# Loading order in the first expert stage: the fourth expert's weights behind the third's, the fifth's ahead of four raw attention pieces

## What is computed

```python
x = x + 0.5 * _L0_ffn_ref(_layernorm(x), gate_w, gate_b, w1, b1, w2, b2)
x = x + _L0_attn_ref(_layernorm(x), Wq, Wk, Wv, Wa, Wg, Wo, ln1..., W1, b1, W2, b2, ln2...)
x = x + 0.5 * _L0_ffn_ref(_layernorm(x), gate_w, gate_b, w1, b1, w2, b2)
```

## Time and profile before

| What | us |
|---|---|
| median of 3 runs | 725.04 (722.64 to 755.42) |
| profiled execution, its own time | 718.21 |
| profiled execution, span from first to last instruction | 716.5 |
| PE busy in the span | 644.8 (90%) |

### The profile page before, as it was taken

How to read it: one execution, slowest core, us unless ns; L and a number is a source line. 1 busy time by engine, 2 the same in 40 slices (tenths; PEclk the granted TensorE clock), 3 DMA queues, 4 the chain that set the end, 5 groups by cost and what they waited for, 6 DMA issues and landing times. The chain is left out here.

```text
span 716.5 us, 11537 instructions
## 1 busy us (share of the span) xinstructions
PE 644.8 (90%) x4307; PEld 572.1 (80%) x4311; DVE 478.7 (67%) x1059; ACT 451.1 (63%) x811; POOL 195.1 (27%) x290
## 2 busy tenths in 40 slices
PE   8999899987779899899999899999996789799993
PEld 5468799565669899799799798898886789489993
DVE  6663500256788989989989989988989776520001
ACT  3425244049689798898899898897797143244440
POOL 6150101320023134235236126215224121420112
PEclk9999999999879999999999999999998798799998
DMA  7959990242001210220121021011011095117700
GB/s 227 339 167 364 306 326 23 72 161 74 29 1 60 75 41 5 73 74 6 70 75 45 31 75 51 24 45 46 0 45 45 1 339 190 52 38 242 250 24 25
DMA packets 48864, 74.07 MB, mean 103 GB/s; under 512 B 4662, under 2 KB 40587, under 8 KB 48744
## 3 DMA queue, kind: packets, MB, share of 16 engines
q1 hardware_dynamic: 44456, 59.84, 25.5%
q0 software_dynamic: 4352, 13.49, 5.3%
HBM read 62.45 MB, written 15.20 MB: 108 GB/s over the span
## 5 line engine op out<-in xcount | busy, mean ns | idle before, releaser
L1639 PE MATMUL bank<-zt_h,w_in_h 128*128 128x512 f32 x192 | 81.4, 424 | 9.6 <-DVE zt_l L1298 5.0
L1639 PE MATMUL bank<-yt_h,w_h 128*128 128x256 f32 x256 | 75.6, 295 | 7.2 <-DVE yt_l L1423 6.4
L982 PE MATMUL bank<-xdt,ring 128*128 128x160 f32 x512 | 75.8, 308 | 4.7 <-DMA ring<-in_L_ffn_w 3.6
L784 DVE SCALAR_TENSOR_TENSOR xo<-bank,gate,xg 128x256 f32<-128x256 f32 x20 | 9.2, 482 | 104.8 <-PE bank L1009 104.8
L982 PEld LDWEIGHTS bank<-xdt,ring 128*128 128x128 f32 x512 | 73.4, 197 | 5.3 <-DMA ring<-in_L_ffn_w 3.8
L1640 PE MATMUL bank<-zt_l,w_in_h 128*128 128x512 f32 x192 | 77.1, 402 | 0.0
L1641 PE MATMUL bank<-zt_h,w_in_l 128*128 128x512 f32 x192 | 76.9, 401 | 0.0
L1639 PE MATMUL bank<-w_h,ht_h 128*128 128x256 f32 x256 | 74.3, 290 | 0.0
L995 PE MATMUL bank<-hid,ring 128*128 128x160 f32 x512 | 72.8, 300 | 1.5 <-DVE idx_s L768 0.7
L1641 PE MATMUL bank<-yt_h,w_l 128*128 128x256 f32 x256 | 73.6, 288 | 0.0
L1640 PE MATMUL bank<-yt_l,w_h 128*128 128x256 f32 x256 | 73.4, 287 | 0.0
(11 more groups left out here) (249 smaller groups left out, 1628.1 us busy)
## 6 DMA issues: line engine op xcount, KB each, us to landing
ring<-in_L_ffn_w SPq DMA_DIRECT2D x32, 1024.0 KB, 9.4
xc<-in_L_attn_x SPq DMA_DIRECT2D x8, 512.0 KB, 4.3
z_mid<-zb POOLq DMA_DIRECT2D x8, 512.0 KB, 3.4
zr<-z_mid SPq DMA_DIRECT2D x16, 256.0 KB, 2.9
xr<-x_mid SPq DMA_DIRECT2D x16, 256.0 KB, 3.6
out<-xq POOLq DMA_DIRECT2D x16, 256.0 KB, 4.2
zb<-x_mid SPq DMA_DIRECT2D x7, 512.0 KB, 5.4
xc<-in_L_attn_W SPq DMA_DIRECT2D x4, 512.0 KB, 8.5
```

The lines of the kernel that those rows point to most:

```text
L784: V.scalar_tensor_tensor(xo[:, a % GT, :], bank[6 + a % 2][:, 0:D], gate[:, a:a + 1], xg[:, a, :], ALU.mult, ALU.add).then_inc(xo_ready, 1)
L982: ins = T.matmul(bank[b][:, 0:CAP], w1_of(s)[:, k, m * P:(m + 1) * P], xdt[:, k, e * CAP:(e + 1) * CAP], start=k == 0, stop=k == KD - 1)
L1639: T.matmul(out, left[0], right[0], start=start, stop=False)
```

## The change

Three things move in `sync_program` of the first expert half, and only there. Nothing that PE, DVE, ACT or POOL execute changes.

1. Expert 3's two DMAs stand right behind expert 2's. The wait for gathers 0 and 1 stood ahead of them and now stands behind them, ahead of `wo_f` and pieces 0 to 3.
2. The copy stands where it stood: behind pieces 0 to 3 and a wait for gathers 0 to 4.
3. Pieces 4 and 5 follow the copy as before. Then come the wait for down 0 and expert 4, and behind these pieces 6 to 9. Expert 5 follows.

```diff
+        def raw_loads(sp, start, stop):
+
+            for n in range(start, stop):
+                if n >= RB:
+                    sp.wait_ge(raw_done, n + 1 - RB)
+                sp.dma_start(raw_view(n), pieces[n][0]).then_inc(raw_in[n % RB], 16)
+
...
-                if first and e == GE - 1:
-                    sp.wait_ge(xg_in[0], 16)
-                    sp.wait_ge(xg_in[1], 16)
                 sp.dma_start(w1_of(s), ew1[e].rearrange("(k p) f -> p k f", p=P)).then_inc(w_in[s], 16)
                 sp.dma_start(w2_of(s), ew2[e].rearrange("(m p) d -> p m d", p=P)).then_inc(w_in[s], 16)
                 if first and e == GE - 1:
 
                     sp.wait_ge(tp_ready, NB * KD)
                     sp.wait_ge(var_ready, NB)
+                    for a in TURN_IN[0]:
+                        sp.wait_ge(xg_in[a], 16)
                     wo = dense_src[5]
                     sp.dma_start(dense["wo_f"][:], wo.rearrange("(k p) n -> p k n", p=P)).then_inc(wo_in, 16)
-                    for n, (piece, _, _) in enumerate(pieces):
-                        if n >= RB:
-                            sp.wait_ge(raw_done, n + 1 - RB)
-                        sp.dma_start(raw_view(n), piece).then_inc(raw_in[n % RB], 16)
-                        if n == RB - 1:
-                            for a in range(GT):
-                                sp.wait_ge(xg_in[a], 16)
-                            sp.dma_start(dst, copy_from).then_inc(copied, 16)
+                    raw_loads(sp, 0, RB)
+                    for a in range(GT):
+                        sp.wait_ge(xg_in[a], 16)
+                    sp.dma_start(dst, copy_from).then_inc(copied, 16)
+                    raw_loads(sp, RB, RB + 2)
+                if first and e == GE:
+                    raw_loads(sp, RB + 2, len(pieces))
```

## The result

The changed kernel is slower: 726.57 us median of 20 runs (724.62 to 730.32), against 723.06 us for the kernel before (median of 20 runs, the three shown at first among them). The ratio is 1.0056, with a 95% interval of 1.0037 to 1.0074. (Ratios and intervals here are estimated from all the runs, so they differ a little from the quotient of two medians, here 1.0048.) Its profiled execution took 724.62 us.

What follows compares the result with a forecast made beforehand. PE, busy for 90% of the span, was taken as the bound, with late expert 4 weights costing a wait and slow clock at up 4. That 5.49 us, all else nothing, took 725.04 to 719.5 us; range 711 to 729.

Steps and rivals of the forecast that it cites:

- What bounds the kernel, and expert 4: At up 4, PE waits for expert 4's late weights, then runs at a slow clock; loading them earlier wins 5.49 us.
- the 3.71 us of waiting: Part of the expert 4 term: up 4 would start at 85.02 us and not at 88.73.
- The 1.78 us of slow clock: Part of the expert 4 term: without the pause before up 4, PE keeps its clock and wins another 1.78 us.
- Issue and landing of expert 4: On SP's queue, expert 4 goes out at about 67.4 us; its second half lands between 78.6 and 83.4, before 85.0.
- Pieces 6 to 9 at nothing: DVE's split before `xo` of tile 0 comes 5.6 us later, covered by downs and ups: cost nothing, otherwise 5.6 us.
- Expert 5's load as the narrowest place: Ahead of up 5: expert 5 lands at the latest at 92.9 us and is wanted at 93.9, so it holds.
- Expert 3 at nothing: Expert 3 lands at 43.4 us, hardly meeting the first gathers: cost taken as nothing, bounds nothing to 4.2 us.
- The copy's place: Before down 0, the copy's packets now overlap gathers 7 to 9: taken as nothing, upper end 5.5 us.
- the upper bound of the same paragraph: Last gathers held back until the copy is done, near 67 us, putting down 0 off by 5.5 us.
- case C: Last gathers held until the copy's packets are through, down 0 late: 7.3 us lost against 5.5 won, 726.8 us, chance 0.16.
- When the copy's packets begin: On SP's queue, the copy's packets begin at about 54 us, 5.6 us sooner than before.

Runs made afterwards that it cites:

- first pair of traces: Profiles of the kernel before and of the changed kernel as first measured: medians 723.06 and 726.57 us.
- experiment 3: Kernel before with only expert 4 moved ahead of pieces 6 to 9, expert 3 at its old place: 718.14 us, ratio 0.9911.
- experiment 12: Kernel before with expert 4 early, expert 3 at its old place, copy behind all ten gathers, repeated on a third chip: 715.47 us, ratio 0.9915.
- second pair: The kernel before and the changed kernel, both unchanged, run again on a third chip: 722.51 and 725.96 us.
- experiment 1: Changed kernel, but the copy waits for all ten gathers and not for five: 715.79 us, ratio 0.9886 against the kernel before.
- 11: Changed kernel with the copy behind all ten gathers, repeated on a third chip: 716.98 us, ratio 0.9927 against the kernel before.
- experiment 10: Changed kernel, unchanged, repeated on a third chip: 725.96 us, ratio 1.0045 against the kernel before.
- 2: Changed kernel with only expert 3 early, expert 4 behind all ten raw pieces again: 725.17 us, ratio 1.0038 against the kernel before.
- 4: Changed kernel with the copy cut into rows of 4 KB and not 64 KB (two DMAs): 720.59 us, ratio 0.9961 against the kernel before.
- 5: Kernel before with one edit, the copy waits for all ten gathers: 725.82 us, ratio 1.0011.
- 7: Changed kernel, but the copy waits for gathers 0 to 6, two more: 721.86 us, ratio 0.9986 against the kernel before.
- 8: Kernel before with expert 4 early, expert 3 at its old place, copy behind all ten gathers, on the second chip: 724.48 us, ratio 0.9987.

## Why the prediction was wrong

**What bounds the kernel, and expert 4.** Right. With expert 4 ahead of pieces 6 to 9, PE's wait for `ring` was gone in every profile. The term was 5.49 us, and 5.50 was measured in the first pair of traces. Experiments 3 and 12, where the gathers cost at most 0.4 us, measured 0.9911 and 0.9915 over the whole run, 6.1 to 6.4 us. Of its two parts, the 3.71 us of waiting is firm. The 1.78 us of slow clock is not: in the second pair it is not there (up 4 took 4.61 us in the kernel before), and the term is (94.11 - 77.13) - 13.26 = 3.72 us.

**Issue and landing of expert 4.** In the changed kernel it was issued at 77.75, not 67.4, since down 0 was late. In experiment 1 it was issued at 69.20, with down 0 1.82 us later than in the first trace. That is the 67.4 expected, moved by the same amount. Its second half, issued at 69.61, landed 12.3 us later, at 81.9, inside the bounds.

**Pieces 6 to 9 at nothing.** Right: PE has no wait for `xo` in any of the profiles. **Expert 5's load as the narrowest place** was right too. It was worked out to hold by 1 us. It held in the changed kernel, and in experiment 12, with the copy issued at 60.32, it failed by 1.01 us.

**Expert 3 at nothing.** Right for gathers 0 and 1 (3.6 and 2.7 us, as before), and its second half landed at 31.63 + 12.0 = 43.6, where 43.4 was worked out. Experiment 12 against 11 shows no value of its own either.

**The copy's place.** Here the prediction failed, in the sentence "I take nothing: the tenth gather alone would land at 53.99 + 2.7 = 56.7, 4.8 us before it is wanted, which is more than one 64 KB packet takes". It priced one turn for each gather. A gather needs three, and so the term put at nothing measured 6.85 us in the first pair of traces (14.02 - 7.17) and 7.86 in the second (15.02 - 7.16), with 2.02 and 1.38 us of slow clock in down 0 behind it. The last gather came in with the end of the copy. That was the upper bound of the same paragraph (5.5 us; its own sum, 54 + 13.8, is 67.8 and not 67, which makes it 6.3), and the case C built on it: 7.3 us lost against 5.5 won, 726.8 us, chance 0.16. The mechanism of C, its place and its sign are what happened. Its size was too small: in the second pair down 0 starts 71.75 - 63.80 = 7.95 us later and then takes 1.38 us more, so 9.33 lost against 3.72 won, 5.6 us at the end of that stretch. Over the whole run the medians differ by 3.5 us in both pairs (726.57 - 723.06 and 725.96 - 722.51). In the second pair's traces 1.86 of the 5.6 us come back at the start of attention, since there the kernel before has a wait that the changed one has not:

```profile
145.96 0.41 DVE L1289 TENSOR_TENSOR b_raw<-b_raw,ln1b_raw 1x256 f32<-1x256 f32 x1 [1.86 <-DMA ln1b_raw<-in_L_attn_ln_bias]
```

That C's 726.8 us lie so near the 726.57 measured is luck. C set a loss of 1.8 us on a median of three runs, 725.04, which was 2 us above that of twenty, and the loss was 3.5 us. The range of 711 to 729 holds the result, but the forecast inside it had the wrong sign.

**When the copy's packets begin.** They were expected 5.6 us sooner, at about 54. They came near 56: between 54 and 55.5 us SP's queue moved 161 packets with 0.15 MB in all, and the first 64 KB packets stand in the stretch from 55.5 us. That is about 3.7 us sooner than the 59.5 of the kernel before.

The error was one of choice rather than of reading. The trace of before had put the copy's first packet at 59.5 and the last gather's landing at 60.3, and so it was known that the two had never met. Between 0 and 5.5 us the lower end was taken, because the gathers had room for one packet. The rule of the Trainium skill that was quoted with it (page "DMA: Bandwidth & Descriptors", section "Queues, rings and completion order": turns change at the end of a packet) pointed to the upper end for a transfer of several packets, and the trace agrees: about 15 packets of POOL's queue pass beside a lump of 16 copy packets. The number of turns could have been read beforehand, from the 96 packets of two gathers between 41 and 46.6 us in the kernel before.

## What to carry to other kernels

A transfer that nobody waits for can still be the one that decides, by what it holds up. Before a load is moved forward, ask what its bytes in the queue had been keeping back: here 2 MB of weights had held a copy off the last gathers, and no wait in the program said so. Make such an order explicit (the change with the copy behind all ten gathers: 0.9886 and 0.9927 of the time before), or leave alone what keeps it (expert 4 moved alone: 0.9911), and keep big packets away from small transfers that are waited for. Where a bound of the trace is open by as much as the gain, price the overlap by turns (packets of the small transfer on each engine times the length of one big packet) and not by bytes. Here that is 3 times 3 us, 9 us. Gather 8 of the changed kernel took 12.4 - 3.3 = 9.1 us more than in experiment 1, and gather 9 of experiment 10 took 15.3 - 3.0 = 12.3 us more than in experiment 11, so the price was met once and exceeded once.

## What was not expected of the hardware

**The early clock varies between executions.** Up to 40 us the changed kernel and the kernel before issue the same on PE, DVE and ACT. In the first trace of the kernel before, the 14 filler matmuls there took this long:

```profile
35.39 4.54 PE L885 MATMUL bank<-iota_p,ones_h 128*128 128x512 bf16 x14
```

In the changed kernel the same row reads:

```profile
35.40 6.01 PE L890 MATMUL bank<-iota_p,ones_h 128*128 128x512 bf16 x14
```

The granted clock was 0.50 (1.2 GHz) until about 38 us in the one and about 41 in the other. In experiments 2, 3 and 4 it was 1.00 through that stretch, and 0.50 around 10 us instead, and in 1, 5, 7 and 11 it was 0.50 in both places. 1.47 us of the changed kernel's first span is this, and not the change. A pause of 3.5 us likewise cost up 4 1.78 us in one trace of the kernel before and 0.10 in the other. The clock can also fall without such a pause. In experiment 3 PE's longest pause between up 1 and down 0 was 0.67 us, and yet the granted clock was 0.59 from 66 to 70 us, and down 0 took 1.7 us more than usual:

```profile
65.39 6.26 PE L1001 MATMUL bank<-hid,ring 128*128 128x160 f32 x32 [0.37 <-DVE idx_s L774]
```

**ACT's gelus in up 0 can be late for no reason that the profile shows.** In the four profiles of one chip up 0 took 5.4 to 9.7 us instead of 4.4. The same kernel (8 and 12) took 20.80 us from up 0 to down 0 on that chip and 14.81 on another. Of the 12 runs on that chip ten were at 723.5 us or above and two at 717.4, so it seems to come and go there. What ACT waits for stays open. Whether the kernel before had it on that chip was not profiled. Its median there, 725.01 us against 723.55 and 722.87 beside the other groups, would fit with it and does not show it.
